# A set-up subtraction on GpSimd from a copy made by ScalarE, in place of VectorE, in a recurrent scan with a 4-bit feed-forward part

## Chip, cores and metric

One Trainium2 chip, one core. The metric is the device time of one launch in microseconds (us). The kernel before has a median of 1521.29 us in 3 runs (1521.10 to 1522.23).

## Reference

The input `x` is (8, 256, 512). A system of 512 coupled oscillators per batch row is integrated over 256 time steps by the classical Runge-Kutta scheme with four stages; each stage needs `tanh(q) @ coupling.T`:

```python
def _derivative(q, p, drive, coupling, bias):
    i_couple = jnp.tanh(q) @ coupling.T
    dq = q - q ** 3 / 3.0 - p + drive + i_couple + bias
    dp = EPSILON * (q + ALPHA - BETA * p)
    return (dq, dp)
# four stages a step; q and p clipped to 20; x is the drive, q's trace the result
```

The trace of `q` then goes through a feed-forward part whose weights are stored as 4-bit floats with a float16 scale for each group of 128:

```python
gate_up = jnp.einsum('bsh,oh->bso', x, w_gu)
h = jax.nn.silu(gate) * up
y = jnp.einsum('bsi,hi->bsh', h, w_down)
rms = jnp.sqrt(jnp.mean(y * y, axis=-1, keepdims=True) + EPS)
return y / rms        # the kernel's output is x plus this
```

## The kernel before

The kernel has two blocks. A block of the program ends when all engines have reached its end; what comes after it starts only then.

The second block is the body. It runs 16 blocks of 16 time steps, each step with four stages (L523 to L544 for TensorE). In each stage ScalarE makes the tanh (L556, L558), VectorE its low part (L590) and the local terms, TensorE multiplies by the coupling (L518), VectorE reduces the sums (L626, L628). The coupling matrix is held in `wscan` three times, for the three step factors in `COEF`, and each time as two float16 tiles of 128 x 2048: a high part, which is the scaled matrix rounded, and a low part, which is the scaled matrix minus the high part. Between the stages' matmuls TensorE works on the feed-forward products (L295, L307) of the block of steps before, by a plan written out ahead. At the end of each block GpSimd computes the root of the mean square from one column (`norm_root`, L333 and L336).

The first block is the set-up, and the change lies in it.

- SyncE's queue (L395 to L414) issues all loads in this order: the state and the bias, unit 0 of the packed weights, the drive, units 1 and 2, the coupling (L411), units 3 to 10. A unit is two transfers, `raw` (L401) and `sc` (L402), into one of three buffers. The load of unit u waits at L399 until VectorE has unpacked unit u - 3.
- VectorE (L433 to L480) prepares the state, then unpacks. One unpack is three instructions over 1536 columns: a shift and a mask in integers (L460), a second shift and mask (L463), and a multiplication by the scales into `wffn` (L466), which frees the buffer. It unpacks units 0 to 3 (L469), makes `with_p` (L474), then makes the three low parts of the coupling (L475 to L478), each after a wait for its high part, and then unpacks units 4 to 10 (L479).
- ScalarE (L422 to L431) sums drive and constants in 16 instructions (L373), waits for the coupling and makes the three high parts (L430), each a scaled copy to float16.
- GpSimd (L417 to L419) writes two small constants and has nothing more to do in the set-up. TensorE has no work in it.

VectorE waits on a semaphore between the instructions of an unpack (`link`, L437 to L440), because the next reads what the one before has written.

Of the kernel before, what the change touches and what calls it, by code (L numbers as in the profile page):

```python
# [21 lines left out]
ALU = mybir.AluOpType  # L22
ACT = mybir.ActivationFunctionType
# [3 lines left out]
B, T, N = 8, 256, 512  # L27
I = 1408
P = 128
KT = N // P  # L30
# [14 lines left out]
S = 65536.0  # L45
CH = DT / 2
AH = CH * EPSILON
COEF = [CH, 2 * CH, CH / 3]
# [150 lines left out]
def program(nc, x, drive, cond_t, coupling_t, bias_t, packed, scales, out):  # L199
    ctx = ExitStack()  # L200

    def sb(name, shape, dt=F32):
        return ctx.enter_context(nc.sbuf_tensor(name, shape, dt))

    def sem(name):
        return ctx.enter_context(nc.semaphore(name))

    with ctx:

        coup = sb("coup", [P, KT, N])  # L210
        wscan = sb("wscan", [P, 3, 2, KT, N], F16)

        hist = [sb(f"hist{i}", [P, KT, STEPS, B]) for i in range(2)]
# [58 lines left out]
        setup_link = sem("setup_link")  # L272
        constants = sem("constants")
        coup_hi = sem("coup_hi")
        sums_set = sem("sums_set")
        dq_w32 = sem("dq_w32")
        stored = sem("stored")
# [91 lines left out]
        def sum_drive(n, half, done):  # L369

            row, c = divmod(n, KT)
            steps = slice(half * HS, (half + 1) * HS)
            nc.scalar.activation(sum_r[:, steps, row, c, :], dr[:, steps, c, :], ACT.Identity,  # L373
                                 bias=constant[:, row, c:c + 1],
                                 scale=float(BY[row, BY_R] * S)).then_inc(done, 1)
# [17 lines left out]
        with nc.Block() as block:  # L393
            @block.sync
            def _(sp):  # L395
                def load_unit(u):
                    b = u % UNPACK_BUFS
                    if u >= UNPACK_BUFS:
                        sp.wait_ge(dq_w32, u - UNPACK_BUFS + 1)  # L399
                    words = packed[u].unsqueeze(1)  # L400
                    sp.dma_start(raw[b][:, :], words.to_broadcast([P // 8, 8, UW])).then_inc(raw_in[b], 16)  # L401
                    sp.dma_start(sc[b][:, :], scales[u:u + 1, :].to_broadcast([P, UW])).then_inc(raw_in[b], 16)  # L402

                sp.dma_start(q_raw[:, :, :], cond_t).then_inc(scan_in, 16)
                sp.dma_start(bias[:, :], bias_t).then_inc(scan_in, 16)
                load_unit(0)
                for half in range(2):
                    sp.dma_start(dr[:, half * HS:(half + 1) * HS], drive[half]).then_inc(loaded, 16)
                load_unit(1)
                load_unit(2)  # L410
                sp.dma_start(coup[:, :, :], coupling_t).then_inc(coup_in, 16)  # L411
                for u in range(3, UNITS):
                    load_unit(u)
                sp.wait_ge(loaded, 32)  # L414

            @block.gpsimd
            def _(pool):  # L417
                nc.gpsimd.iota(shift[:, :], [[0, 1]], base=P - 1, channel_multiplier=-1).then_inc(iota_done, 1)
                nc.gpsimd.memset(mhalf[:, :], -0.5)  # L419

            @block.scalar
            def _(act):  # L422
                nc.scalar.preload_act_table(ACT.Silu)
                act.wait_ge(loaded, 32)
                act.wait_ge(constants, ROWS)
                for n in range(SUM_R_PARTS):
                    sum_drive(n, 0, sums_set)
                act.wait_ge(coup_in, 16)
                for n, coef in enumerate(COEF):
                    nc.scalar.activation(wscan[:, n, 0], coup[:, :, :], ACT.Copy,  # L430
                                         scale=coef * S).then_inc(coup_hi, 1)  # L431

            @block.vector  # L433
            def _(dve):
                count = [0]

                def link(ins):  # L437
                    count[0] += 1
                    ins.then_inc(setup_link, 1)
                    dve.wait_ge(setup_link, count[0])  # L440

                dve.wait_ge(scan_in, 32)
                nc.vector.tensor_scalar(p_state[:, :, :], q_raw[:, :, :], -P_SHIFT, S / P_UNIT, ALU.add, ALU.mult)
                nc.vector.tensor_scalar(hist[1][:, :, STEPS - 1, :], q_raw[:, :, :], S, None, ALU.mult)
                for row in range(ROWS):
                    nc.vector.tensor_scalar(constant[:, row], bias[:, :], float(BY[row, BY_R] * S),
                                            float(BY[row, BY_ONE] * S), ALU.mult, ALU.add).then_inc(constants, 1)
                dve.wait_ge(constants, ROWS)
                dve.wait_ge(iota_done, 1)

                link(nc.vector.tensor_scalar(shift[:, :], shift[:, :], 7, 2, ALU.bitwise_and,
                                             ALU.logical_shift_left))
                link(nc.vector.tensor_copy(q_raw[:, :, :], hist[1][:, :, STEPS - 1, :]))

                def unpack(u):

                    b = u % UNPACK_BUFS
                    bits = nib[u % 2]
                    dve.wait_ge(raw_in[b], 32 * (u // UNPACK_BUFS + 1))
                    link(nc.vector.tensor_scalar(bits[:, :], raw[b][:, :], shift[:, 0:1], -(1 << 28),  # L460
                                                 ALU.logical_shift_left, ALU.bitwise_and))

                    link(nc.vector.tensor_scalar(bits[:, :], bits[:, :], 3, 0x8E000000 - (1 << 32),  # L463
                                                 ALU.arith_shift_right, ALU.bitwise_and))
                    fp4 = bits[:, :].bitcast(F16).rearrange("p (n two) -> p n two", two=2)[:, :, 1]
                    nc.vector.scalar_tensor_tensor(wffn[:, u, :], fp4, FP4_BITS, sc[b][:, :],  # L466
                                                   ALU.mult, ALU.mult).then_inc(dq_w32, 1)

                for u in range(UNPACK_BUFS + 1):  # L469
                    unpack(u)  # L470

                dve.wait_ge(sums_set, SUM_R_PARTS)
                p_rows = p_state[:, :, :].unsqueeze(1).to_broadcast([P, ROWS, KT, B])
                nc.vector.scalar_tensor_tensor(with_p[:, :], p_rows, P_ALL, sum_r[:, 0], ALU.mult, ALU.add)  # L474
                for n, coef in enumerate(COEF):  # L475
                    dve.wait_ge(coup_hi, n + 1)
                    nc.vector.scalar_tensor_tensor(wscan[:, n, 1], coup[:, :, :], coef * S, wscan[:, n, 0],
                                                   ALU.mult, ALU.subtract)  # L478
                for u in range(UNPACK_BUFS + 1, UNITS):  # L479
                    unpack(u)  # L480

# [237 lines left out]
        def pool_block(pool, now, before, ffn, rest):  # L719
            for s in range(STAGES):  # L720
                for plan, f, _, at in jobs(now, before, ffn, rest, s):
                    if at == plan.norm_root:
                        norm_root(pool, f)
            if before:


                pool.wait_ge(now.clipped, HS)
                pool.wait_ge(now.xres_in, 16)
                pool.wait_ge(now.down_done, 2)
                pool.wait_ge(now.drive_lo, 16)  # L730
                if rest:
                    pool.wait_ge(before.out_ready, KT)
                nc.gpsimd.sem_clear(before.range)
                pool.sem_inc(now.other_cleared, 1)
# [115 lines left out]
```

## Time and profile before

| | |
|---|---|
| median of 3 runs | 1521.29 us (1521.10 to 1522.23) |
| profiled execution | 1519.87 us |
| its span, first to last instruction | 1518.0 us |
| granted TensorE clock, mean | 0.999 |
| TensorE busy (matmul) | 1424.1 us, 94% |
| VectorE busy | 1434.8 us, 95% |
| ScalarE busy | 718.9 us, 47% |
| GpSimd busy | 12.2 us, 1% |
| end of the set-up's last VectorE instruction | 65.0 us |

How to read it: busy time is the sum of the profiled instructions of an engine, and the span is 1.87 us shorter than the execution's own time. Names: PE is TensorE, PEld its weight loads, DVE is VectorE, ACT is ScalarE, POOL is GpSimd, SP is SyncE and SPq its queue. L430 is line 430 of the kernel before. In a timeline a row is start, duration, engine, line, operation, tiles written and read, their sizes, the number of instructions merged in the row, and in brackets how long the engine had been idle before and what ended that. A DMA share is the mean busy share of the core's 16 DMA engines.

### The profile page before, as it was taken

How to read it: one execution, taken by the hardware profiler on the slowest of the kernel's cores; microseconds unless marked ns; L12 is line 12 of the kernel's file. 1: busy time of each engine (PE TensorE's matmuls, PEld its weight loads, DVE VectorE, ACT ScalarE, POOL GpSimd, SP SyncE). 2: the span in 40 equal slices, each digit the busy share in tenths (PEclk: the TensorE clock that was granted, in tenths of full speed). 3: DMA queues.
4: the chain of work that ended last, by engine and by line, in shares of the span. 5: the costliest groups of instructions: out<-in, count | busy, mean ns of one | idle time of the engine just before them, and what ended most of it. 6: DMA issues, size and time to landing. Idle time of an engine off the chain costs nothing.

```text
span 1518.0 us, 90291 instructions
## 1 busy us (share of the span) xinstructions
PE 1424.1 (94%) x36992; PEld 1408.7 (93%) x36992; DVE 1434.8 (95%) x10781; ACT 718.9 (47%) x4836; POOL 12.2 (1%) x38
## 2 busy tenths in 40 slices
PE   0277999999999999999999999999999999999998
PEld 0166999999999999999999999999999999999998
DVE  6999999999999999999999999999999999999991
ACT  2144445445454544545454454545445455544541
POOL 0000000000000000000000000000000000000000
PEclk9999999999999999999999999999999999999999
DMA  9500000000000000000000000000000000000000
GB/s 243 138 7 4 15 7 8 22 8 21 4 8 21 8 21 8 21 4 7 21 8 22 7 22 4 8 21 8 22 8 21 7 4 22 7 21 8 22 4 22
DMA packets 13520, 32.67 MB, mean 22 GB/s; under 512 B 1712, under 2 KB 6064, under 8 KB 12976
## 3 DMA queue, kind: packets, MB, share of 16 engines
q1 hardware_dynamic: 13104, 26.89, 6.7%
q8 instruction: 289, 4.73, 1.3%
q14 instruction: 127, 1.04, 0.2%
HBM read 22.69 MB, written 4.19 MB: 18 GB/s over the span
## 4 chain that ended last, share of the span: by engine, by line
PE 89%; DVE 5%; ACT 0%; issue 0%; POOLq 0%; DVEq 0%; POOL 0%; ACTq 0%
PE scan_ps L518 53%; PE gu_ps L295 22%; PE y_ps L307 14%; DVE th L590 1%; DVE q_stage L626 1%; DVE with_q L584 1%; DVE q_stage L628 1%; DVE q_sq L594 0%; DVE scan_ps L602 0%; DVE p_part L584 0%; DVE q_cub L597 0%; DVE with_p L584 0%; ACT th L556 0%; DVE q_raw L628 0%; DVE q_raw L626 0%
## 5 line engine op out<-in xcount | busy, mean ns | idle before, releaser
L518 PE MATMUL scan_ps<-th,wscan 128*128 128x32 f16 (+1 forms) x32768 | 1015.9, 175 | 87.6 <-ACT th L556 87.0
L518 PEld LDWEIGHTS scan_ps<-th,wscan 128*128 128x128 f16 x32768 | 937.9, 96 | 102.6 <-ACT th L556 95.1
L556 ACT ACTIVATE th<-q_stage 128x16 f16<-128x16 f32 x1536 | 318.5, 207 | 527.6 <-DVE q_stage L626 527.6
L295 PE MATMUL gu_ps<-hist,wffn 128*128 128x128 f32 x2816 | 503.3, 284 | 0.0
L295 PEld LDWEIGHTS gu_ps<-hist,wffn 128*128 128x128 f32 x2816 | 393.9, 192 | 0.0
L590 DVE TENSOR_TENSOR th<-t,th 128x16 f16<-128x16 f32 x2048 | 352.6, 172 | 1.1 <-ACT t L558 0.6
L307 PE MATMUL y_ps<-wffn,h 128*128 128x128 f32 x1408 | 323.6, 313 | 0.0
L558 ACT ACTIVATE t<-q_stage 128x16 f32<-128x16 f32 x1536 | 305.8, 199 | 0.0
L556 ACT ACTIVATE th<-q_raw 128x16 f16<-128x16 f32 x512 | 106.2, 207 | 220.8 <-DVE q_raw L626 182.6
L307 PEld LDWEIGHTS y_ps<-wffn,h 128*128 128x128 f32 x1408 | 209.5, 189 | 0.4 <-DVE h L323 0.4
L373 ACT ACTIVATE sum_r<-dr,constant 128x64 f32<-128x64 f32 x528 | 174.1, 332 | 7.8 <-DMA dr<-drive 7.8
L626 DVE TENSOR_REDUCE q_stage<-scan_ps 128x16 f32<-128x48 f32 x768 | 158.4, 206 | 18.5 <-PE scan_ps L518 12.3
L628 DVE TENSOR_REDUCE q_stage<-scan_ps 128x16 f32<-128x48 f32 x768 | 159.3, 207 | 0.3
L602 DVE SCALAR_TENSOR_TENSOR scan_ps<-with_q,q_cub 128x32 f32<-128x32 f32 x768 | 151.5, 197 | 0.0
L594 DVE SCALAR_TENSOR_TENSOR q_sq<-q_stage 128x32 f32<-128x32 f32 x768 | 145.6, 190 | 3.2
L584 DVE SCALAR_TENSOR_TENSOR p_part<-p_part,q_stage 128x32 f32<-128x32 f32 x768 | 143.3, 187 | 0.0
L597 DVE SCALAR_TENSOR_TENSOR q_cub<-q_sq,q_stage 128x32 f32<-128x32 f32 x768 | 142.5, 186 | 0.0
L584 DVE SCALAR_TENSOR_TENSOR with_q<-q_stage,with_q 128x32 f32<-128x32 f32 x768 | 140.6, 183 | 0.0
L584 DVE SCALAR_TENSOR_TENSOR with_q<-hist,with_p 128x32 f32<-128x32 f32 x768 | 140.5, 183 | 0.0
L558 ACT ACTIVATE t<-q_raw 128x16 f32<-128x16 f32 x512 | 102.0, 199 | 0.0
L584 DVE SCALAR_TENSOR_TENSOR with_p<-p_state,sum_r 128x128 f32<-128x128 f32 x256 | 74.8, 292 | 0.0
L323 DVE SCALAR_TENSOR_TENSOR h<-gu_ps,silu 128x128 f32<-128x128 f32 x176 | 49.5, 281 | 23.5 <-ACT silu L316 23.1
(33 smaller groups left out, 539.3 us busy)
## 6 DMA issues: line engine op xcount, KB each, us to landing
raw<-packed SPq DMA_DIRECT2D x11, 768.0 KB, 9.0
dr<-drive SPq DMA_DIRECT2D x34, 128.0 KB, 2.5
sc<-scales SPq DMA_DIRECT2D x11, 384.0 KB, 9.3
xres<-x SPq DMA_DIRECT2D x16, 256.0 KB, 3.5
out<-osb SPq DMA_DIRECT2D x16, 256.0 KB, 2.9
coup<-coupling_t SPq DMA_DIRECT2D x1, 1024.0 KB, 15.0
q_raw<-cond_t SPq DMA_DIRECT2D x1, 16.0 KB, 1.6
bias<-bias_t SPq DMA_DIRECT2D x1, 2.0 KB, 1.7
```

Source lines behind the costliest of these rows:

```text
L295: i = nc.tensor.matmul(gu_ps[b][:, half * P:(half + 1) * P], wffn[:, u, j * P:(j + 1) * P], hist[1 - f.parity][:, kt].rearrange("p t b -> ...
L307: i = nc.tensor.matmul(y_ps[f.parity][:, cols], h32[b][:, :], wffn[:, u, 2 * KT * P:][:, cols], start=(u == 0 and j == 0), stop=(u == UNIT ...
L373: nc.scalar.activation(sum_r[:, steps, row, c, :], dr[:, steps, c, :], ACT.Identity, bias=constant[:, row, c:c + 1], scale=float(BY[row, B ...
L518: i = nc.tensor.matmul(to if both else to[:, 0], wscan[:, w, part, kt, cols], moving if both else moving[:, 0], start=first, stop=last, sk ...
L556: nc.scalar.activation(th[s % 2][:, c, 0, :], q[:, c, :], ACT.Tanh, scale=1.0 / S).then_inc(now.tanh_hi, 1)
L558: nc.scalar.activation(t32[:, c, :], q[:, c, :], ACT.Tanh, scale=1.0 / S).then_inc(now.tanh_32, 1)
L584: return local(nc.vector.scalar_tensor_tensor(to, x, factor, base, ALU.mult, ALU.add))
L590: nc.vector.tensor_tensor(th[s % 2][:, c, 1, :], t32[:, c, :], th[s % 2][:, c, 0, :], ALU.subtract).then_inc(now.tanh_lo, 1)
L594: return local(nc.vector.scalar_tensor_tensor(q_sq[:, :, :], q, CUBE[i], q, ALU.mult, ALU.mult))
L602: nc.vector.scalar_tensor_tensor(local_ps, halves(linear[i]), UNIT[i], halves(q_cub[:, :, :]), ALU.mult, ALU.add).then_inc(now.first_half, 1)
L626: nc.vector.tensor_reduce(q_next[:, 0:HC, :], three[0], AX.X, ALU.add).then_inc(now.q_ready, 1)
L628: nc.vector.tensor_reduce(q_next[:, HC:KT, :], three[1], AX.X, ALU.add).then_inc(now.q_ready, 1)
```

## The change

In the set-up ScalarE makes, beside each high part, the same scaled copy of the coupling in float32, into one of two new buffers `scaled`. GpSimd subtracts the high part from it and writes the low part. VectorE's three subtractions are taken out. Two semaphores are added: `coup_scaled` (ScalarE to GpSimd) and `coup_low` (GpSimd to ScalarE). From the third step factor on ScalarE waits until the buffer is free; that wait stands ahead of the high part. Each of the new buffers takes 8 KB in each partition. No transfer is added, removed or moved.

```diff
         coup = sb("coup", [P, KT, N])
+        scaled = [sb(f"scaled{i}", [P, KT, N]) for i in range(2)]
...
         coup_hi = sem("coup_hi")
+        coup_scaled = sem("coup_scaled")
+        coup_low = sem("coup_low")
...
             def _(pool):
                 nc.gpsimd.iota(shift[:, :], [[0, 1]], base=P - 1, channel_multiplier=-1).then_inc(iota_done, 1)
                 nc.gpsimd.memset(mhalf[:, :], -0.5)
+                for n in range(len(COEF)):
+                    pool.wait_ge(coup_scaled, n + 1)
+                    pool.wait_ge(coup_hi, n + 1)
+                    nc.gpsimd.tensor_tensor(wscan[:, n, 1], scaled[n % 2][:, :, :], wscan[:, n, 0],
+                                            ALU.subtract).then_inc(coup_low, 1)
...
                 for n, coef in enumerate(COEF):
+                    if n >= 2:
+                        act.wait_ge(coup_low, n - 1)
                     nc.scalar.activation(wscan[:, n, 0], coup[:, :, :], ACT.Copy,
                                          scale=coef * S).then_inc(coup_hi, 1)
+                    nc.scalar.activation(scaled[n % 2][:, :, :], coup[:, :, :], ACT.Copy,
+                                         scale=coef * S).then_inc(coup_scaled, 1)
...
                 nc.vector.scalar_tensor_tensor(with_p[:, :], p_rows, P_ALL, sum_r[:, 0], ALU.mult, ALU.add)
-                for n, coef in enumerate(COEF):
-                    dve.wait_ge(coup_hi, n + 1)
-                    nc.vector.scalar_tensor_tensor(wscan[:, n, 1], coup[:, :, :], coef * S, wscan[:, n, 0],
-                                                   ALU.mult, ALU.subtract)
                 for u in range(UNPACK_BUFS + 1, UNITS):
                     unpack(u)
```

## Rows read from the trace of the kernel before

**Rows 1.** The page, chain that ended last: shares of the span by engine
```profile
PE 89%; DVE 5%; ACT 0%; issue 0%; POOLq 0%; DVEq 0%; POOL 0%; ACTq 0%
```

**Rows 2.** Waits of the first 66 us, and the queue of SyncE's in the first 70
```profile
PE scan_ps L518 <- ACT th L556: 65.6, 1, 65.6
...
DVE nib L460 <- DMA sc<-scales: 12.9, 7, 5.0
...
SPq L401 <- DVE wffn L466: 36.4, 8, 9.3
```

**Rows 3.** Timeline of the set-up: start us, us, engine, line, op, tiles
```profile
21.57 5.51 ACT L430 ACTIVATE wscan<-coup 128x2048 f16<-128x2048 f32 x3 [7.89 <-DMA coup<-coupling_t]
...
26.21 1.02 DVE L460 TENSOR_SCALAR nib<-raw,shift 128x1536 int32<-128x1536 int32 x1 [3.56 <-DMA sc<-scales]
...
30.04 0.55 SPq L401 DMA_DIRECT2D raw<-packed  x1
30.13 6.69 DVE L477 SCALAR_TENSOR_TENSOR wscan<-coup,wscan 128x2048 f16<-128x2048 f32 x3
...
40.57 0.55 SPq L401 DMA_DIRECT2D raw<-packed  x1
41.16 0.59 SPq L402 DMA_DIRECT2D sc<-scales  x1
...
52.28 1.02 DVE L460 TENSOR_SCALAR nib<-raw,shift 128x1536 int32<-128x1536 int32 x1 [0.58 <-DMA sc<-scales]
...
61.19 1.02 DVE L460 TENSOR_SCALAR nib<-raw,shift 128x1536 int32<-128x1536 int32 x1 [0.52 <-DMA sc<-scales]
...
63.23 1.76 DVE L466 SCALAR_TENSOR_TENSOR wffn<-nib,sc 128x1536 f32<-128x1536 f16 x1
...
65.29 0.21 ACT L556 ACTIVATE th<-q_raw 128x16 f16<-128x16 f32 x1 [38.21 <-PEq L393]
```

**Rows 4.** Groups of instructions from 0 to 65.1 us: busy us, mean ns
```profile
L466 DVE SCALAR_TENSOR_TENSOR wffn<-nib,sc 128x1536 f32<-128x1536 f16 x11 | 19.3, 1758 | 0.4
L460 DVE TENSOR_SCALAR nib<-raw,shift 128x1536 int32<-128x1536 int32 x11 | 11.2, 1017 | 12.9 <-DMA sc<-scales 12.9
L463 DVE TENSOR_SCALAR nib<-nib 128x1536 int32<-128x1536 int32 x11 | 10.6, 960 | 0.4
L477 DVE SCALAR_TENSOR_TENSOR wscan<-coup,wscan 128x2048 f16<-128x2048 f32 x3 | 6.7, 2283 | 0.0
...
L451 DVE TENSOR_SCALAR shift<-shift 128x1 int32<-128x1 int32 x1 | 0.2, 154 | 0.0
```

**Rows 5.** Stretches of the set-up: busy time by engine, clock, DMA share, GB/s
```profile
26.00:39.00 13.00, 0.00 (x0) 0.00 (x0) 12.65 (x10) 1.08 (x1) 0.00 (x0) 1.00 1.02 246
39.00:42.00 3.00, 0.00 (x0) 0.00 (x0) 2.97 (x3) 0.00 (x0) 0.00 (x0) 1.00 0.14 37
...
42.00:43.00 1.00, 0.00 (x0) 0.00 (x0) 0.96 (x2) 0.00 (x0) 0.00 (x0) 1.00 0.87 276
```

**Rows 6.** Groups of GpSimd's instructions over the span: busy us, mean ns
```profile
L336 POOL TENSOR_TENSOR rinv<-meansq,mhalf 128x1 f32<-128x1 f32 x16 | 8.8, 551 | 1.3
L333 POOL TENSOR_SCALAR meansq<-sumsq 128x1 f32<-128x1 f32 x16 | 3.1, 192 | 1499.3 <-ACT junk L328 1499.3
```

**Rows 7.** Timelines: GpSimd near 258 us, VectorE near 258 and near 264 us
```profile
258.50 0.55 POOL L336 TENSOR_TENSOR rinv<-meansq,mhalf 128x1 f32<-128x1 f32 x1
...
258.46 0.18 DVE L584 SCALAR_TENSOR_TENSOR with_q<-q_stage,with_q 128x32 f32<-128x32 f32 x1
...
258.97 0.17 DVE L590 TENSOR_TENSOR th<-t,th 128x16 f16<-128x16 f32 x1
...
263.89 0.18 DVE L584 SCALAR_TENSOR_TENSOR with_q<-q_stage,with_q 128x32 f32<-128x32 f32 x1
...
264.41 0.17 DVE L590 TENSOR_TENSOR th<-t,th 128x16 f16<-128x16 f32 x1
```

**Rows 8.** Tile sc in the first 70 us: time of its transfers from issue to landing
```profile
DMA to landing us min/median/max: 6.4/9.3/12.9
```

## The prediction, made before the changed kernel was run

> **What bounds the kernel now.** I read the chain of waits first. It is almost all TensorE: 89% of the span, in the matmuls of the scan and of the feed-forward part [rows 1]. That is the body of the kernel, after the set-up, and the change touches none of it. So I went to the waits of the first 66 us. TensorE's first matmul waits 65.6 us, VectorE waits 12.9 us for transfers, and SyncE's queue waits 36.4 us for VectorE to free a load buffer [rows 2]. The whole set-up is therefore serial time in front of a body that keeps its length: each microsecond by which the set-up ends earlier or later is a microsecond of the result, and the only question is when the last engine leaves the set-up block.
>
> The timeline shows who that is [rows 3]. VectorE unpacks eleven units of weights, numbers 0 to 10; unit 3 starts at 26.21, unit 8 at 52.28, unit 10 at 61.19, and the last instruction ends at 63.23 + 1.76 = 64.99 us. The first tanh starts at 65.29, and before it ScalarE had waited 38.2 us for the block's end. One unpack keeps VectorE for 3.75 us (1.02, 0.96 and 1.76 us [rows 4]). Between units 3 and 4 lie the three subtractions of the coupling, 30.13 to 36.82. Before units 8 and 10 VectorE is idle until a transfer lands. So at the end the DMA sets the pace, not VectorE: 52.28 to 61.19 is two units, 4.5 us each, against 3.75 us of VectorE's work.
>
> **What the removal gives.** Three instructions of 2.28 us [rows 4], 6.7 us in the timeline, go. This is not worth 6.7 us, because the last unit lands when the DMA has moved it. The view of stretches shows what the DMA lost: full work is a share of 1.02 (26 to 39 us); from 39 to 42 us the share is 0.14, from 42 to 43 it is 0.87 [rows 5]. That is (3 x 0.88 + 0.15) / 1.02 = 2.7 us of idle DMA. It comes about because the load of unit 7 is issued only at 40.57, when the unpack of unit 4 has given its buffer back [rows 3]. Without the subtractions that unpack would start when its unit has landed, near 31 us (a unit takes (61.19 - 26.21 - 2.7) / 7 = 4.6 us, on from 26.2), and end near 34.6; the load of unit 7 would be queued 6 us earlier, behind a unit that keeps the DMA busy until about 39 [rows 5]. The gap closes, and the next loads, issued near 39 and 44 us, stay some 3 us ahead of the queue. If nothing else happens the last unit lands 2.7 us earlier and VectorE ends 2.7 us earlier. Were the whole of 39 to 42 us lost, and 0.15 us after it, it would be 3.1; I take 2.7 and keep 3.1 as the end of the range.
>
> **What is added on ScalarE.** Three more copies of 128x2048, at 1.84 us from start to start (5.51 us for three [rows 3]). The order becomes high 0 at 21.6, scaled 0 at 23.4, high 1 at 25.2, scaled 1 at 27.1, high 2 at 28.9, scaled 2. High 2 waits for the first GpSimd subtraction, so that the buffer is free; behind it on ScalarE only scaled 2 is queued. ScalarE stands idle for 38.2 us after 27.1, so 5.5 us and that wait cost nothing, as long as GpSimd is through by some 50 us. No DMA is added or moved, and SP's queue keeps its order.
>
> **What is added on GpSimd.** Three subtractions of 128x2048, the first from 25.3 us. GpSimd has nothing else to do before the block's end. The trace has no wide GpSimd instruction. It has two of one column: 0.192 us, which is 1.25 times VectorE's 0.154 us for an instruction on one column, and 0.551 us, 3.6 times [rows 6, 4]. Applied to VectorE's 2.28 us for the same tile that gives 2.85 and 8.2 us as ends. I take twice VectorE's time, 4.6 us: it is nearer the lower end, as an instruction of one column is mostly fixed cost, while the two inputs for each element remain. The GPSIMD Engine Reference of the Trainium skill (section on performance versus the Vector engine) gives 4.5 us for such a tensor_tensor on float32; no run here shows it yet, and with it the sum below would be 0.3 us less. As cover GpSimd has 25.3 to some 62 us, so alone it could take 12 us an instruction before it were the end.
>
> **The unknown that decides: does VectorE keep its pace beside GpSimd?** The one-column rows bound it from below. GpSimd's 0.55 us at 258.50 runs beside VectorE's short instructions, six of which start from 258.46 to 258.97; five microseconds later, beside nothing, the same six start from 263.89 to 264.41 [rows 7]. That is 0.51 and 0.52 us: no delay, so the lower end is nothing. But one column is read at once; that row says little of 2048 columns that are streamed for microseconds. From above: the two engines exclude each other for the length of an instruction. What makes me lean to this end is VectorE's rate. Its two integer instructions take 0.96 to 1.02 us for 1536 columns, its two-input ones 1.76 us for 1536 and 2.28 for 2048, that is 1.03 ns a column at the margin [rows 4]. So the integer ones fetch columns at almost double rate, and the third of an unpack fetches two tiles: each of the three takes two streams out of memory, and GpSimd's would be a third one.
>
> The Trainium skill says this outright: by SBUF — State Buffer, section "Who interferes with whom", GpSimd and VectorE share a pair of ports as an exclusive lock, held for the whole instruction by whoever starts first, against a VectorE instruction in a two-port mode or with two inputs in SBUF. By that rule this change is a loss and without it a small gain; the one-column row does not show it, and no row of the trace refutes it at this width.
>
> **The sum, with exclusion turn by turn.** GpSimd starts at 25.3, ahead of VectorE at 26.2. GpSimd 25.3 to 29.9; first instruction of unpack 3 to 30.9; GpSimd (its input was ready at 29) to 35.5; second to 36.5; GpSimd to 41.1; third to 42.9. Unpack 3 ends at 42.9 in place of 30.0, and only then is unit 6 issued. The DMA has run dry near 35, when unit 5 has landed (26.2 + 2 x 4.6 = 35.4). From issue to landing through an empty queue: 0.6 us to the second issue and 6.4 us from there, the shortest in this stretch [rows 3, 8], so 7.0. Unit 6 lands at 49.9, and units 7 to 10, issued meanwhile, 4.5 us apart: 67.9. With the last unpack 71.7, against 65.0: **6.7 us longer**. Each microsecond more or less in GpSimd's price moves this by 3: 1.5 us at 2.85, 17.5 at 8.2.
>
> The profiled execution took 1519.87 us (span 1518.0, 1.87 around it), and the median of the runs is 1521.29, 1.42 above it. A shift of 6.7 us brings the profiled time to 1526.6 and the median to **1528.0 us**. About 0.2%, 3.0 us, is what a measurement can tell from no change.
>
> **Rivals.**
> - No exclusion (0.32): VectorE's rows keep 1.02, 0.96 and 1.76 us, the gap in the DMA closes, 1518.6 us (1518.2 with 3.1). For it: the one-column rows. It lies at the bound of 0.2%, so a third of its chance is faster.
> - Exclusion, but VectorE keeps its turn when it has work (0.13): only the first GpSimd instruction is in its way (3.7 us, ends at 33.7, almost hidden by the queue), the second slips in when VectorE first waits for a unit, near 49, and pushes the last three unpacks to 53.4 + 11.2 = 64.6; the third gets in only behind them, to 69.2, and the block's end waits for it: 4.2 us slower, 1525.5 us. This one makes GpSimd the bound at the very end; it decides if the second and third start after 48 us.
> - Mild blocking (0.08): a cheap GpSimd instruction, below 3.3 us, or only the two integer instructions held back briefly: -0.6 to +3 us, about 1522.
> - GpSimd far dearer than twice VectorE (0.05): at 8 us under exclusion 17 us longer, 1538 us.
> - That the work does not leave VectorE is excluded by the diff. My own case has 0.42.
>
> **The numbers.** Slower by over 0.2%: 0.42, 0.10 of the second rival and 0.05 of the last, 0.57. Faster: a third of the first rival, 0.10. The rest, 0.33, within 0.2%. The range goes from 1518.2, the no-exclusion end, to 1530.5, which is my case with GpSimd at 5.4 us; it leaves out dearer prices. The likeliest case by itself has 1525 to 1530.5.
>
> **What would show it.** Right: VectorE's rows of unpack 3 start late or stretch to GpSimd's length, its waits in the first 66 us grow by about 13 us, the load of unit 6 is issued near 43 us, DMA shares are near zero from 36 to 44 us, and the first tanh comes near 72 us. Wrong: unpack 3 ends at 30.0, the load of unit 7 is issued near 34.6, the DMA has no gap at 40 us and the first tanh is at 62.6. GpSimd's rows above 5.4 or below 3 us would make the price wrong, and a third GpSimd instruction after 60 us would show the second rival. Any difference in the stage pace after the set-up would be outside this account.

## The result: 4.3 us slower, and the profile after

The changed kernel has a median of 1525.48 us in 8 runs (1525.24 to 1525.87), the kernel before 1521.19 us in 8 runs (1520.78 to 1522.23): 4.3 us more, 1.0027 times as long, with an interval of 1.0017 to 1.0037. It was forecast at 1528.0, between 1518.2 and 1530.5, slower. The profiled execution took 1525.48 us and its span is 1523.7 us. Of the difference of 5.7 us between the two profiled spans the set-up holds 4.5 (below). The rest, 1.2 us, lies in the body: from the first tanh to the end it is 1523.7 - 69.83 = 1453.9 us, against 1518.0 - 65.29 = 1452.7 before. The change has no part in that rest. A second profile of the same kernel, experiment e8, has 1522.7 - 70.19 = 1452.5. And the profiled execution of the kernel before, 1519.87 us, is shorter than all eight of its timed runs; a run at their median with the same set-up would have a body of 1521.19 - 1.87 - 65.29 = 1454.0 us, as long as that of the changed kernel.

The timeline of the changed kernel's set-up comes first; it answers to [rows 3], and its columns are the same. L426 is GpSimd's subtraction; L472, L475 and L478 are the three instructions of an unpack.

```profile
25.79 4.07 DVE L472 TENSOR_SCALAR nib<-raw,shift 128x1536 int32<-128x1536 int32 x1 [3.37 <-DMA sc<-scales]
...
29.08 1.91 ACT L440 ACTIVATE wscan<-coup 128x2048 f16<-128x2048 f32 x1 [0.59 <-POOL wscan L426]
29.90 4.70 DVE L475 TENSOR_SCALAR nib<-nib 128x1536 int32<-128x1536 int32 x1
...
34.64 5.49 DVE L478 SCALAR_TENSOR_TENSOR wffn<-nib,sc 128x1536 f32<-128x1536 f16 x1
...
40.16 0.55 SPq L404 DMA_DIRECT2D raw<-packed  x1
40.25 1.01 DVE L472 TENSOR_SCALAR nib<-raw,shift 128x1536 int32<-128x1536 int32 x1
...
67.78 1.76 DVE L478 SCALAR_TENSOR_TENSOR wffn<-nib,sc 128x1536 f32<-128x1536 f16 x1
...
69.83 0.22 ACT L564 ACTIVATE th<-q_raw 128x16 f16<-128x16 f32 x1 [37.03 <-PEq L396]
```

The three subtractions in the timeline of GpSimd alone:

```profile
24.98 4.07 POOL L426 TENSOR_TENSOR wscan<-scaled,wscan 128x2048 f16<-128x2048 f32 x1 [23.99 <-ACT scaled L442]
...
29.00 4.79 POOL L426 TENSOR_TENSOR wscan<-scaled,wscan 128x2048 f16<-128x2048 f32 x1
...
33.75 4.77 POOL L426 TENSOR_TENSOR wscan<-scaled,wscan 128x2048 f16<-128x2048 f32 x1
```

Read the two together. Unpack 3 meets the three subtractions, and its instructions take 4.07, 4.70 and 5.49 us in place of 1.02, 0.96 and 1.76 [rows 4]. The engine is not called idle in that time: a blocked instruction's wait stands inside its row and counts as busy. The first subtraction is done at 29.05, when ScalarE's waiting copy starts; VectorE's first instruction ends 0.8 us later, at 29.86. That is its own 1.02 us less 0.2: it gets its turn some 0.2 us before GpSimd's row ends. GpSimd's second row starts at 29.00 but is 0.72 us longer than its first: it in turn stands behind VectorE. At 33.79 and 38.52 the same happens again. No other unpack is stretched, as the tile nib shows over the first 75 us (minimum, median and maximum in ns of 11 each; the maximum is that of unpack 3):

```profile
L472 DVE TENSOR_SCALAR nib<-raw,shift x11: 1008/1020/4074, 8.7 to 65.7; 128x1536 int32<-128x1536 int32 x11
L475 DVE TENSOR_SCALAR nib<-nib x11: 960/960/4702, 9.8 to 66.8; 128x1536 int32<-128x1536 int32 x11
L478 DVE SCALAR_TENSOR_TENSOR wffn<-nib,sc x11: 1757/1759/5491, 10.8 to 67.8; 128x1536 f32<-128x1536 f16 x11
```

What this does to the transfers is in the stretches (the columns of [rows 5]) and in the waits of SyncE's queue:

```profile
26.00:34.00 8.00, 0.00 (x0) 0.00 (x0) 7.97 (x2) 6.20 (x4) 8.00 (x3) 1.00 1.01 244
34.00:42.00 8.00, 0.00 (x0) 0.00 (x0) 7.93 (x5) 0.00 (x0) 4.51 (x1) 1.00 0.09 20
42.00:65.00 23.00, 0.00 (x0) 0.00 (x0) 20.43 (x17) 0.00 (x0) 0.00 (x0) 1.00 1.02 252
```

```profile
SPq L404 <- DVE wffn L478: 40.6, 8, 16.5
```

Unit 6 is issued at 40.16, when unpack 3 has given a buffer back, and not at 30.04. SyncE's queue waits 40.6 us for load buffers, 16.5 of them at once; before it was 36.4 and 9.3 [rows 2]. The DMA stands still for (8 x (1.02 - 0.09)) / 1.02 = 7.3 us between 34 and 42, where the kernel before lost 2.7 us in its gap from 39 to 43. That is 4.6 us more, and the first tanh comes 69.83 - 65.29 = 4.5 us later.

### The profile page after: what moved, and what is told of

It is laid out like the page before. It is cut to its first block, busy times and chain, and to the rows that moved or that the text cites. A ratio compares the mean times of both kernels' runs of the same rounds, so it can differ in the third digit from the quotient of the medians.

```text
span 1523.7 us, 90297 instructions
## 1 busy us (share of the span) xinstructions
PE 1425.4 (94%) x36992; PEld 1409.4 (92%) x36992; DVE 1440.4 (95%) x10778; ACT 724.4 (48%) x4839; POOL 25.8 (2%) x41
## 4 chain that ended last, share of the span: by engine, by line
PE 90%; DVE 5%; ACT 0%; issue 0%; POOLq 0%; DVEq 0%; POOL 0%; ACTq 0%
PE scan_ps L526 53%; PE gu_ps L298 23%; PE y_ps L310 14%; DVE th L598 1%; DVE q_stage L634 1%; DVE with_q L592 1%; DVE q_stage L636 0%; DVE q_sq L602 0%; DVE scan_ps L610 0%; DVE p_part L592 0%; DVE q_cub L605 0%; ACT th L564 0%; DVE with_p L592 0%; DVE q_raw L636 0%; DVE q_raw L634 0%; DVE hist L621 0%
```

## The experiments

Theory A: GpSimd and VectorE exclude each other for the length of an instruction and take turns. Theory B: both share the memory's bandwidth and slow each other while they work. A third question is what VectorE's freed time is worth. e1 to e4 ran on one chip and e5 to e8 on another, each beside runs of the kernel before on the same chip: 1519.40 us in 27 runs for e1 to e4, 1519.79 us in 16 runs for e5 to e8. Differences are against these. In the code cuts the line that takes out what is replaced is not always shown, and `...` stands for lines left out.

**e1, neither engine subtracts.** GpSimd's three instructions are gone, and with them ScalarE's wait for them. ScalarE fills the low part with a second scaled copy; the subtraction is left out of the computation.

```diff
-                for n in range(len(COEF)):            # in the GpSimd block, all of it
...
-                    nc.scalar.activation(scaled[n % 2][:, :, :], coup[:, :, :], ACT.Copy,
-                                         scale=coef * S).then_inc(coup_scaled, 1)
+                    nc.scalar.activation(wscan[:, n, 1], coup[:, :, :], ACT.Copy,
+                                         scale=coef * S / 4096).then_inc(coup_scaled, 1)
```

> Leaves out the subtraction: ScalarE writes a second scaled copy where the low part belongs, and neither VectorE nor GpSimd has work for it, so this is the changed kernel without GpSimd's three instructions. Theory A (GpSimd and VectorE exclude each other, turn by turn): VectorE's unpack rows all keep 1.02, 0.96 and 1.76 us, the DMA's gap of 2.7 us closes, the first tanh starts near 62.6 us and the median falls by 2.7 us, to 1518.5. Rival (the transfers hide VectorE's subtractions altogether, so nothing was to be gained): 1521.2. Rival (the second copy of ScalarE slows VectorE's unpack, not GpSimd): unpack of unit 3 stays stretched and the time near 1525.

Measured: 1516.19 us, 3.2 us below the kernel before, ratio 0.9980 (0.9971 to 0.9989). Timeline of e1:

```profile
25.79 1.02 DVE L465 TENSOR_SCALAR nib<-raw,shift 128x1536 int32<-128x1536 int32 x1 [3.43 <-DMA sc<-scales]
...
34.23 0.55 SPq L404 DMA_DIRECT2D raw<-packed  x1
...
61.94 0.22 ACT L557 ACTIVATE th<-q_raw 128x16 f16<-128x16 f32 x1 [29.85 <-PEq L396]
```

The unpack is undisturbed beside six copies on ScalarE, unit 7 is issued at 34.23 instead of 40.57, and the first tanh is at 61.94. So the time that VectorE was to be spared is worth some 3 us, not 6.7, and ScalarE's copies do no harm. GpSimd's three instructions turn this gain into the loss.

**e2, each subtraction in two halves.**

```diff
-                    nc.gpsimd.tensor_tensor(wscan[:, n, 1], scaled[n % 2][:, :, :], wscan[:, n, 0],
-                                            ALU.subtract).then_inc(coup_low, 1)
+                    for kt in range(0, KT, 2):
+                        k = slice(kt, kt + 2)
+                        nc.gpsimd.tensor_tensor(wscan[:, n, 1, k], scaled[n % 2][:, k, :], wscan[:, n, 0, k],
+                                                ALU.subtract).then_inc(coup_low, 1)
...
-                        act.wait_ge(coup_low, n - 1)
+                        act.wait_ge(coup_low, 2 * (n - 1))
```

> Each of GpSimd's three subtractions is cut in two halves. Theory A (exclusive, turn by turn): each VectorE instruction of unpack 3 waits for one half instead of a whole, some 2 us each, so unpack 3 ends near 34.6 us instead of 40.1, and three more VectorE instructions behind it are held back by the other halves; the load of unit 7 is issued near 44 us, the last unit lands near 64.5 and the median is near 1524.2, 1.3 us below the changed kernel. Theory B (both engines share the memory's bandwidth and slow each other as long as both work): nothing depends on the size of the pieces, the three instructions of unpack 3 keep 4.1, 4.7 and 5.5 us, and the median stays at 1525.5 or above by the halves' own overhead.

Measured: 1522.83 us, 3.4 us over the kernel before, 1.0021 (1.0012 to 1.0030). Timeline of VectorE in e2 from unpack 3 on:

```profile
25.80 2.23 DVE L474 TENSOR_SCALAR nib<-raw,shift 128x1536 int32<-128x1536 int32 x1 [3.44 <-DMA sc<-scales]
...
28.06 2.76 DVE L477 TENSOR_SCALAR nib<-nib 128x1536 int32<-128x1536 int32 x1
...
30.85 3.56 DVE L480 SCALAR_TENSOR_TENSOR wffn<-nib,sc 128x1536 f32<-128x1536 f16 x1
...
34.34 2.20 DVE L488 SCALAR_TENSOR_TENSOR with_p<-p_state,sum_r 128x128 f32<-128x128 f32 x1
...
36.47 2.87 DVE L474 TENSOR_SCALAR nib<-raw,shift 128x1536 int32<-128x1536 int32 x1
39.37 2.76 DVE L477 TENSOR_SCALAR nib<-nib 128x1536 int32<-128x1536 int32 x1
```

Unpack 3 ends at 34.4 (34.6 was expected). The second instruction waits 2.76 - 0.96 = 1.80 us; behind a whole subtraction it waited 4.70 - 0.96 = 3.74. The wait follows the size of the piece, which Theory B does not give. `with_p`, an instruction of 0.28 us, is held for 1.92 us as well: a short VectorE instruction pays the same wait as a long one. It does not wait for the result of the multiplication before it, so the two engines take turns there too, without such a wait between VectorE's instructions. The six waits come to 10.4 us, as much as the three of the changed kernel (3.05 + 3.74 + 3.73 = 10.5), and the time is only about 1 us shorter. The buffer of unpack 3 is free at 34.4 instead of 40.1, but then unpack 4 gives back its own only at 43.9: over 34 to 46 us the DMA share is 0.45, in the changed kernel 0.39, which is 6.7 against 7.4 us of standing still.

**e3, GpSimd last.** One wait more, so that nothing runs beside GpSimd.

```diff
+                pool.wait_ge(dq_w32, UNITS)
                 for n in range(len(COEF)):
```

> GpSimd's subtractions wait until VectorE has unpacked all units, so nothing runs beside them. Theory A: GpSimd's own price is what its first instruction showed, 4.07 us; the 4.79 and 4.77 us of the others hold a wait for VectorE's turn. All three are then near 4.1 us, VectorE's unpack is undisturbed and ends near 62.3, and the set-up ends near 74.6 us: 9.3 us over the kernel before, 1530.5. Theory B (bandwidth shared, own price lower than any row): below 3.5 us each, 1528.5. Rival (4.8 us is the undisturbed price): 76.6 us and 1532.5.

Measured: 1528.97 us, 9.6 us over the kernel before, 1.0061 (1.0046 to 1.0077). From e3: two rows of the timeline at unpack 3, the subtractions with minimum, median and maximum in ns, and the first tanh:

```profile
26.08 1.02 DVE L473 TENSOR_SCALAR nib<-raw,shift 128x1536 int32<-128x1536 int32 x1 [3.50 <-DMA sc<-scales]
26.85 1.90 ACT L443 ACTIVATE scaled<-coup 128x2048 f32<-128x2048 f32 x1
```

```profile
L427 POOL TENSOR_TENSOR wscan<-scaled,wscan x3: 4054/4054/4066, 62.3 to 70.3; 128x2048 f16<-128x2048 f32 x3
```

```profile
74.69 0.22 ACT L565 ACTIVATE th<-q_raw 128x16 f16<-128x16 f32 x1 [4.62 <-PEq L396]
```

GpSimd's own price is 4.05 us. The 4.79 and 4.77 us in the changed kernel hold 0.7 us of waiting for VectorE. ScalarE's float32 copy, the same as in the changed kernel, runs beside unpack 3 here, and the unpack keeps its pace; this closes the one gap that e1 left, whose second copy was in float16.

**e4, only an order of VectorE changed.** The kernel before, with VectorE's first subtraction ahead of unpack 3, where it waits for a transfer, the second behind `with_p` and the third behind unpack 5.

```diff
+                def low(n):                           # waits for high part n, subtracts as before
...
-                for u in range(UNPACK_BUFS + 1):
+                for u in range(UNPACK_BUFS):
                     unpack(u)
+                low(0)
+                unpack(UNPACK_BUFS)
...
+                low(1)
                 for u in range(UNPACK_BUFS + 1, UNITS):
                     unpack(u)
+                    if u == UNPACK_BUFS + 2:
+                        low(2)
```

> The kernel before with VectorE's subtractions moved only: the first one stands ahead of unpack 3, where VectorE waits for a transfer anyway (23.4 to 25.8 us), the second behind with_p, the third behind unpack 5. If the 2.7 us of idle DMA are all there is to win, VectorE itself can win them: no gap near 40 us, first tanh near 62.6, 1518.5. Rival: the two subtractions that still lie between unpacks leave a shorter gap, 1 to 2 us gained, 1519.5 to 1520.

Measured: 1516.82 us, 2.6 us below the kernel before, 0.9983 (0.9974 to 0.9992). Timeline and one stretch of e4:

```profile
23.24 2.29 DVE L471 SCALAR_TENSOR_TENSOR wscan<-coup,wscan 128x2048 f16<-128x2048 f32 x1 [0.86 <-ACT wscan L430]
25.92 1.02 DVE L460 TENSOR_SCALAR nib<-raw,shift 128x1536 int32<-128x1536 int32 x1 [0.39 <-DMA sc<-scales]
...
62.19 0.21 ACT L561 ACTIVATE th<-q_raw 128x16 f16<-128x16 f32 x1 [35.39 <-PEq L393]
```

```profile
39.00:42.00 3.00, 0.00 (x0) 0.00 (x0) 3.00 (x3) 0.00 (x0) 0.00 (x0) 1.00 1.03 224
```

The DMA's gap is closed with the subtractions still on VectorE, with the whole computation, and the time is within 0.6 us of e1, which leaves the subtraction out. This version is faster than the kernel before, with an interval that leaves out 1, and the changed kernel is slower than the kernel before.

**e5, which VectorE instructions are blocked.** In the changed kernel three more VectorE instructions stand ahead of unpack 3, their results unused.

```diff
-                for u in range(UNPACK_BUFS + 1):
+                for u in range(UNPACK_BUFS):
                     unpack(u)
+                dve.wait_ge(coup_scaled, 1)
+                for k in range(2):
+                    link(nc.vector.tensor_reduce(sumsq[:, 0:1], coup[:, k, :], AX.X, ALU.add))
+                link(nc.vector.tensor_scalar(junk[:, :], coup[:, 2, :], 1.0, None, ALU.mult))
+                unpack(UNPACK_BUFS)
```

> Ahead of unpack 3, as soon as GpSimd's first subtraction starts (near 25 us), VectorE gets three more instructions of 512 float32 columns: two reductions, which have one input and ran in no faster mode in this case, and one multiplied copy, which may run at double rate as the integer instructions do. Theory A1 (only VectorE instructions that take two streams are excluded): the reductions take 0.5 to 0.7 us each beside GpSimd, the copy waits for GpSimd's end near 29 us and so shows 2.5 to 3.5 us. Theory A2 (any VectorE instruction is excluded): the first reduction already takes some 4 us and the second one too. The time is near that of the changed kernel either way, within 1 us.

Measured: 1524.18 us in one run, 4.4 us over the kernel before. Timeline of e5:

```profile
25.62 1.41 DVE L485 TENSOR_REDUCE sumsq<-coup 128x1 f32<-128x512 f32 x2 [2.74 <-ACT scaled L442]
25.68 13.00 POOL L426 TENSOR_TENSOR wscan<-scaled,wscan 128x2048 f16<-128x2048 f32 x3 [24.69 <-ACT scaled L442]
27.07 2.96 DVE L486 TENSOR_SCALAR junk<-coup 128x512 f32<-128x512 f32 x1
...
30.07 4.70 DVE L472 TENSOR_SCALAR nib<-raw,shift 128x1536 int32<-128x1536 int32 x1
```

Two reductions of 512 columns take 0.70 us each beside GpSimd's first subtraction, not the 4 us of a blocked one. No run has such a reduction alone, but an estimate from [rows 4] gives the same: 1.03 ns a column and some 0.18 us fixed, as the two-input rows have them, make 0.71 us. The copy right behind them ends at 30.03, soon after that subtraction, and shows 2.96 us. So not every VectorE instruction is shut out. The reduction has one input and goes at the single rate. The integer instructions and the copy have one input too, but are of the kind that goes at almost double rate; the others that were held have two.

**e6, GpSimd only writes.** The subtraction is left out; GpSimd fills the same tiles with zeros.

```diff
-                    nc.gpsimd.tensor_tensor(wscan[:, n, 1], scaled[n % 2][:, :, :], wscan[:, n, 0],
-                                            ALU.subtract).then_inc(coup_low, 1)
+                    nc.gpsimd.memset(scaled[n % 2][:, :, :], 0.0)
+                    nc.gpsimd.memset(wscan[:, n, 1], 0.0).then_inc(coup_low, 1)
```

> Leaves out the subtraction: where GpSimd subtracted it now fills the same tiles, scaled and the low part, with zeros, two instructions for each step factor that write 2048 columns and read nothing. Theory A1 (the exclusion goes by streams of reads and of writes apart): the integer instructions of unpack 3 that meet a fill are stretched by its length, the multiplication by the scales with its two inputs and one output keeps 1.76 us even where it meets one. Theory A3 (GpSimd's instruction holds everything): the multiplication is stretched as well. The fills are short, 1 to 2 us each, so the set-up ends between 62.3 and 65 us, at or below the kernel before.

Measured: 1517.60 us in one run, 2.2 us below the kernel before. Timeline of e6:

```profile
24.84 1.80 POOL L426 MEMSET scaled<- 128x2048 f32 x1 [23.85 <-ACT scaled L442]
...
26.58 2.62 POOL L427 MEMSET wscan<- 128x2048 f16 x1
27.49 2.52 DVE L475 TENSOR_SCALAR nib<-nib 128x1536 int32<-128x1536 int32 x1
29.14 2.61 POOL L426 MEMSET scaled<- 128x2048 f32 x1
...
30.05 1.76 DVE L478 SCALAR_TENSOR_TENSOR wffn<-nib,sc 128x1536 f32<-128x1536 f16 x1
```

An undisturbed fill takes 1.80 us (the first one, at 24.84). The integer instruction at 27.49 shows 2.52 us in place of 0.96: it is held until the fill ends, near 29.2. The fill that is entered at 29.14 is held by it, runs to 31.75, and so covers the multiplication by the scales from 30.05 on; that one has two inputs and keeps its 1.76 us. Against a GpSimd instruction that only writes, the two-input instruction is free, and the double-rate one is not. So reads and writes are excluded apart. This rests on the rows of one run, in which it happens twice: the multiplication of unpack 4 too keeps 1.76 us beside a fill (36.90, with the fill from 36.00 to 38.61).

**e7, each subtraction in eight pieces** of 256 columns, a loop like that of e2.

```diff
...
+                    for i in range(8):
+                        c = slice(i % 2 * 256, i % 2 * 256 + 256)
+                        nc.gpsimd.tensor_tensor(wscan[:, n, 1, i // 2, c], scaled[n % 2][:, i // 2, c],
+                                                wscan[:, n, 0, i // 2, c], ALU.subtract).then_inc(coup_low, 1)
```

> Each of GpSimd's subtractions is cut in eight pieces of 256 columns. Theory A (exclusive, turn by turn): each VectorE instruction waits for one piece, about 0.5 us, so an unpack takes some 5.3 us from unit 3 on, for as long as pieces are left (some seven unpacks). Unpack 3 ends near 31.2 us, the set-up near 66.6: 2.9 us below the changed kernel and some 1.5 over the kernel before. Theory B (bandwidth shared): the same time as the changed kernel or the halves, whatever the pieces.

Measured: 1519.11 us, 0.7 us below the kernel before, 0.9996 (0.9987 to 1.0005): no difference. Timeline of e7, unpack 3 and the first tanh:

```profile
25.86 1.32 DVE L474 TENSOR_SCALAR nib<-raw,shift 128x1536 int32<-128x1536 int32 x1 [3.55 <-DMA sc<-scales]
...
27.21 1.31 DVE L477 TENSOR_SCALAR nib<-nib 128x1536 int32<-128x1536 int32 x1
28.55 2.11 DVE L480 SCALAR_TENSOR_TENSOR wffn<-nib,sc 128x1536 f32<-128x1536 f16 x1
...
64.69 0.21 ACT L566 ACTIVATE th<-q_raw 128x16 f16<-128x16 f32 x1 [26.41 <-PEq L396]
```

GpSimd's pieces, minimum, median and maximum in ns:

```profile
L428 POOL TENSOR_TENSOR wscan<-scaled,wscan x24: 670/1379/2179, 25.1 to 58.6; 128x256 f16<-128x256 f32 x24
```

The form is that of Theory A and Theory B is out; my size was off. I had expected 0.5 us a piece and an end near 66.6. The wait behind a piece is 1.31 - 0.96 = 0.35 us. With 1.80 behind 1024 columns and 3.74 behind 2048 this is a line: 1.9 ns a column less 0.13 us a piece. Part of a GpSimd instruction lies outside the exclusion: undisturbed it takes 0.67 us for 256 columns, 2.13 for 1024 (the first half in e2) and 4.05 for 2048 (e3), each 0.3 us more than the wait behind it, and 24 pieces hide 24 such parts. VectorE is now the bound from unpack 3 to the end: 64.40 - 25.86 = 38.5 us is eight unpacks of 3.72, `with_p` and 23 waits, 8.5 us together. The kernel still loses nothing against the one before, because the waits are spread: unpack 3 ends at 30.6, the DMA has no gap (a share of 1.03 from 34 to 42 us), and each later unpack takes 4.8 us with its three waits, hardly more than the 4.6 us that the transfer of a unit takes in any case.

**e8, the changed kernel again.** No edit.

> The changed kernel once more, unchanged, so that it stands beside the others on this chip: 1.0027 to 1.003 times the kernel before, 4.1 to 4.6 us more, with unpack 3 at 4.1, 4.7 and 5.5 us.

Measured: 1524.15 us, 4.4 us over the kernel before on that chip, 1.0030 (1.0018 to 1.0041). The comparison holds in this second set of runs.

## Why the prediction was right, and where its size was off

- **What bounds the kernel**: right. The body kept its length in every profile (1452.0 to 1452.7 us from the first tanh to the end, but for the 1453.9 named above), and the change of the set-up was that of the result to within some 0.6 us in each.
- **What the removal gives**: 2.7 us, with 3.1 as the end. e1 shows 3.2 us in the medians, between 1.7 and 4.4 by its interval. In the traces, from the start of unpack 3 to the first tanh, it is 61.94 - 25.79 = 36.15 us against 65.29 - 26.21 = 39.08, 2.9 us. Right within its bounds.
- **ScalarE's copies and its wait cost nothing**: right. The wait was 0.59 us.
- **VectorE does not keep its pace**: this was the deciding step, and I took the end that no row of the trace before showed. It is right: turn by turn, GpSimd first, as the sum had it. The argument from rates (the double-rate instruction takes two streams) is supported by e5 and e6; that a fill, which reads nothing, holds a double-rate instruction too was not in it. The Trainium skill's SBUF — State Buffer, section "Who interferes with whom", says the same in these points: the turn for a whole instruction (3.74 us behind 2048 columns), a reduction free (0.70 us), a two-input instruction held by a reading GpSimd (5.49 us) and free beside a writing one (1.76 us). It gives the whole instruction as the length of the turn; measured, 0.3 us of each GpSimd instruction lie outside (e7). The one-column row that spoke against it [rows 7] does not contradict: by the line in e7 a piece of one column makes no wait.
- **GpSimd's price**: the term that was mis-sized. I took 4.6 us, twice VectorE's time. Undisturbed it is 4.05 us (e3). In the sum's own steps GpSimd's three turns (the later two from VectorE's end to its own) took 4.07, 3.93 and 3.92 us, 1.9 us less than 3 x 4.6, and VectorE's three between and after them 3.2 us instead of 3.8, because each began before GpSimd's row had ended. That is 2.4 to 2.5 us, as much as lies between the 6.7 us forecast and the 4.3 measured. Unpack 3 ended at 40.1 where the sum had 42.9; 0.3 us of that is GpSimd's earlier start, and the four units behind unit 6, 4.6 us apart and not 4.5, took some of it back. The Trainium skill's GPSIMD Engine Reference, section "Performance versus the Vector engine", has 4.5 us for float32, which is over the measured 4.05 us too; here one input and the output are float16.
- **The second rival** (VectorE keeps its turn) named 1525.5 us and so hit the median. It is wrong all the same: its third GpSimd instruction was to start after 60 us, and it starts at 33.75. A number that fits is not a mechanism that fits.
- **The signs**: one did not come. VectorE's waits were to grow by about 13 us and grew by 0.5, from 12.9 to 13.4 us; the 10.5 us stand inside its rows instead. The DMA was at zero from 35 to 41 us, not to 44, and the first tanh came at 69.83, not near 72, both by the smaller price.

## What to carry to other kernels

Before moving work from VectorE to GpSimd, look at what VectorE runs beside it. Beside a GpSimd instruction that reads and writes wide tiles, VectorE's two-input and double-rate instructions stood still in every run here; 6.7 us of VectorE's time were bought with 10.5 us of waits inside its rows, at the very place where a load buffer had to be freed. Before moving work off an engine, look for idle time of that same engine: a change of order won nearly the whole gain (2.6 us in e4, 3.2 in e1), because what was scarce was not VectorE's time but the moment at which it gave a buffer back. If GpSimd must be used beside VectorE, small pieces cost less than large ones (e2, e7): in e7 no load buffer was held back for long.

## What was unexpected about the hardware

A blocked instruction shows as busy, on either engine: VectorE's busy time went up from 1434.8 to 1440.4 us (1438.7 in e8) although three instructions were taken from it. The wait goes by GpSimd's piece and hardly by the instruction that waits: one of 0.28 us was held for 1.92 us (e2), one of 0.96 us for 1.80. And cutting an instruction in eight made it cheaper for its neighbour, 8.5 us of waits in e7 against 10.5 us in the changed kernel; I had expected the same total or more. Why some 0.3 us of each piece lie outside the exclusion was not tried.
